# A graph network on one NeuronCore: block numbers of a chunk's groups loaded by one instruction at the chunk's head

## What is computed

```python
def forward(x):
    for layer in (transformer_conv, three_gat_convs, gatv2_with_kan, dot_attention):
        h = jnp.maximum(_layernorm(x, axis=-1), 0.0)
        x = x + layer(h)
    return x
# each edge layer, over all edges (src -> dst):
#   e     = score(node[dst], node[src])
#   alpha = exp(e - segment_max(e)[dst]); denom = segment_sum(alpha, dst)
#   out   = segment_sum(alpha[..., None] * value[src], dst) / denom
```

## Time and profile before

| | |
|---|---|
| median of 3 runs | 7453.76 us (7451.57 to 7457.46) |
| profiled execution, its own time | 7448.15 us |
| its span in the trace | 7446.4 us |
| granted TensorE clock, mean | 0.755 |
| TensorE busy | 4521.2 us (61%) |
| VectorE busy | 4569.1 us (61%) |
| ScalarE busy | 1779.9 us (24%) |
| GpSimd busy | 5124.9 us (69%) |

### The profile page before, as it was taken

How to read it: one execution, slowest core, us unless ns; L and a number is a source line. 1 busy time by engine, 2 the same in 40 slices (tenths; PEclk the granted TensorE clock), 3 DMA queues, 4 the chain that set the end, 5 groups by cost and what they waited for, 6 DMA issues and landing times. The chain is left out here.

```text
span 7446.4 us, 117629 instructions
## 1 busy us (share of the span) xinstructions
PE 4521.2 (61%) x21806; PEld 3437.6 (46%) x21806; DVE 4569.1 (61%) x15575; ACT 1779.9 (24%) x4978; POOL 5124.9 (69%) x5206
## 2 busy tenths in 40 slices
PE   3888887545555645555534444455766675677776
PEld 2544554433344433433433333444655564566665
DVE  5888887445555735555644444476777776566666
ACT  2888887200000000000010000043111111111111
POOL 5777773177777567777767777735777773777775
PEclk7999999777777767777766666666777777677677
DMA  3666664156666556666544444402444443566665
GB/s 88 164 166 165 163 165 129 41 178 184 187 185 185 164 164 186 187 185 183 183 121 135 138 132 132 138 30 66 129 130 130 129 130 99 173 184 180 181 182 154
DMA packets 659335, 1107.41 MB, mean 149 GB/s; under 512 B 233389, under 2 KB 383719, under 8 KB 658533
## 3 DMA queue, kind: packets, MB, share of 16 engines
q0 software_dynamic: 205312, 519.10, 26.9%
q1 hardware_dynamic: 450070, 579.16, 24.4%
q10 hardware_dynamic: 3280, 1.64, 0.1%
HBM read 997.90 MB, written 101.51 MB: 148 GB/s over the span
## 5 line engine op out<-in xcount | busy, mean ns | idle before, releaser
L516 POOL DMA_INDIRECT gat_ring<-tab,gat_ixb x2562 | 2459.8, 960 | 865.4 <-issue 738.3
L929 PE MATMUL gat_sc_ps<-gat_ring,gat_plain 128*128 128x264 f32 (+1 forms) x5124 | 1463.8, 430 | 42.9 <-DVE gat_ring L701 27.8
L516 POOL DMA_INDIRECT dot_ring<-tab,dot_ixb x854 | 831.5, 974 | 356.9 <-issue 237.7
L929 PEld LDWEIGHTS gat_sc_ps<-gat_ring,gat_plain 128*128 128x128 f32 x5124 | 985.1, 230 | 175.8 <-issue 83.4
L516 POOL DMA_INDIRECT conv_ring<-tab,conv_ixb x854 | 821.8, 962 | 310.0 <-issue 233.0
L516 POOL DMA_INDIRECT gatv_ring<-tab,gatv_ixb x854 | 838.0, 981 | 271.1 <-issue 244.2
L942 PE MATMUL gat_mx_ps<-ident,gat_lg 128*104 128x128 f32 x111 | 46.2, 416 | 1537.7 <-DVE gat_lg L757 1537.7
L746 DVE TENSOR_REDUCE gat_ex_sum<-gat_ex_ps 128x192 f32<-128x576 f32 (+1 forms) x114 | 81.8, 719 | 1428.8 <-SPq L525 1428.3
L701 DVE TENSOR_TENSOR gat_ring<-gat_ring,gat_p_ps 128x520 f32<-128x520 f32 (+1 forms) x1281 | 760.1, 594 | 4.1
L1052 ACT ACTIVATE gat_ring<-gat_low_own 128x96 f32<-128x96 f32 (+2 forms) x111 | 41.3, 372 | 2980.0 <-DVE gat_low_own L791 2783.6
L942 PEld LDWEIGHTS gat_mx_ps<-ident,gat_lg 128*104 128x104 f32 x111 | 17.7, 160 | 1570.4 <-issue 1570.4
(11 more groups left out here) (453 smaller groups left out, 7947.3 us busy)
## 6 DMA issues: line engine op xcount, KB each, us to landing
gat_plain<-d_plain SPq DMA_DIRECT2D x318, 512.0 KB
gat_turned<-d_turned SPq DMA_DIRECT2D x318, 256.0 KB
d_plain<-xs SPq DMA_DIRECT2D x427, 128.0 KB
gatv_plain<-d_plain SPq DMA_DIRECT2D x106, 512.0 KB
dot_plain<-d_plain SPq DMA_DIRECT2D x106, 512.0 KB
gat_ring<-tab,gat_ixb POOLq DMA_INDIRECT x2562
conv_rel_row<-d_rel SPq DMA_DIRECT2D x107, 256.0 KB
d_turned<-conv_ohT SPq DMA_DIRECT2D x427, 64.0 KB
```

The lines of the kernel that those rows point to most:

```text
L516: gp.indirect_dma_start(out=ring[:, r, t, 0:width], out_offset=None, in_=table[:, :], in_offset=bass.IndirectOffsetOnAxis(ap=ixb[:, r, t:t ...
L929: last = pe.matmul(sc_ps[:, m % SCB, 0:F], which[:, u, :], rows, start=(u == 0), stop=(u == 1))
```

## The change

In every layer but conv, TensorE and VectorE load the block numbers of all groups of a chunk with one instruction, values_load_multi_w_load_instructions, and keep them as values until the chunk is done with. The bounds 0 to 24 are given for it as before. TensorE does so in expand of the chunk's group 0; VectorE in shrink_sums of the chunk, whose own number is the first of them, and add takes its numbers from the list. In shrink_sums the load comes ahead of the wait for `shrink`, in conv too, where it stays a load of one number.

```diff
@@ message_pass
+    def blocks_of(ch, engine):
+
+        _, values = nc.values_load_multi_w_load_instructions(T.blk[0:1, BASE[ch]:BASE[ch + 1]], engines=[engine],
+                                                             min_val=0, max_val=NB - 1)
+        return values
+
@@ VectorE
+            block_at = {}
@@ add
                 m = BASE[i] + g
-                block_of = v.value_load(T.blk[0:1, bass.ds(m, 1)], min_val=0, max_val=NB - 1)
+                if conv:
+                    block_of = v.value_load(T.blk[0:1, bass.ds(m, 1)], min_val=0, max_val=NB - 1)
+                else:
+                    block_of = block_at[i][g]
                 v.wait_ge(s("scat"), m + 1)
@@ shrink_sums
+                if conv:
+                    block_of = v.value_load(T.blk[0:1, bass.ds(BASE[ch], 1)], min_val=0, max_val=NB - 1)
+                else:
+                    block_at.pop(ch - 2, None)
+                    block_at[ch] = blocks_of(ch, mybir.EngineType.DVE)
+                    block_of = block_at[ch][0]
                 v.wait_ge(s("shrink"), ch + 1)
-                block_of = v.value_load(T.blk[0:1, bass.ds(BASE[ch], 1)], min_val=0, max_val=NB - 1)
                 v.nop(nofuse=True)
@@ TensorE
+            block_at = {}
+
             def expand(i, r, g, use):
 
                 n = BASE[i] + g
-                block_of = pe.value_load(T.blk[0:1, bass.ds(n, 1)], min_val=0, max_val=NB - 1)
+                if conv:
+                    block_of = pe.value_load(T.blk[0:1, bass.ds(n, 1)], min_val=0, max_val=NB - 1)
+                else:
+                    if g == 0:
+                        block_at.pop(i - 1, None)
+                        block_at[i] = blocks_of(i, mybir.EngineType.PE)
+                    block_of = block_at[i][g]
                 mine = nd[:, bass.ds(block_of, 1), :].rearrange("p o w -> p (o w)")
```

## The result

Median of five runs 7491.3 us (7483.7 to 7494.2), against 7451.6 us (7443.4 to 7457.5) for the kernel before beside it: 40 us more, ratio 1.0054, 95% interval 1.0041 to 1.0066. The forecast was 7507 us, which is 53 us over the 7453.8 it started from; "slower" had the chance 0.75. The profiled run has a span of 7488.2 us, 41.8 more than the profiled run before, about the difference of the medians, so the two traces are laid side by side. Each is a single execution: conv, where only one load was moved, takes 1353.7 to 1358.8 us over the traces of before, the change and e1 to e8, so 1 or 2 us of a layer can't be told from nothing.

The account below looks back on a forecast made before the run. GpSimd's issue of gathers was taken to pace the five layers; gatv2's middle +27 and the tails +26 made +53 us, 7507 us on the 7453.76 median. The range was 7440 to 7780, the main case 7465 to 7560 (chance 0.42).

Parts of the forecast that it names:

- GpSimd's pace sets the middles: Five layers after conv: gather issue, 1.26 us a gather, paces them; TensorE and VectorE savings mid-layer are worth nothing.
- One load for n words, 0.31 + 0.057 a further word: Chunk heads on TensorE and VectorE: one load costs 0.31 us plus 0.057 us for each further word.
- Rival 1: Chunk heads: words load one after another, 0.305 us each; sum +386 us, 7840 us; chance 0.34.
- Checks kept, 0.28 us a number: Chunk heads, both engines: each number keeps its check and assert, about 0.28 us with gaps.
- gatv2, middle, +27: gatv2 before its tail: heads add 7.4 us a chunk against 6.6 available, short 0.8 in 34 chunks, +27 us.
- half of the 2.1 counts: gatv2's middle: of 2.1 us issue a chunk, half is recoverable, TensorE's clock being high about half the time.
- Rival 3: Heads are long but almost all covered, by gatv2's slack and tail waits for scatters: 7453 to 7469 us, chance 0.15.
- The prediction's slack: VectorE's idle time per chunk, taken as waits for gathered rows: 12.9 us in GAT, 8.6 dot, 5.6 gatv2.
- Tails, +26: Last four chunks: heads less removed issue and waits, 6.4 us gatv2, 5.7 dot, 6.9 each first two GAT, 0 third.
- Rest, 0: Conv, node stages, and GpSimd's and SyncE's queues: no cost or gain, 0 us.
- two thirds of rival 1's price: Cheaper further words in the heads: gatv2 gives 142 us, dot 10, tails 48; 7654 us.
- the tails give 20: Lower bound, load 0.31 us whatever n: gatv2's middle covered, 7474 us; upper, 0.1 us a word: tails 33, 7548 us.

Follow-up runs that it names:

- e1: The change taken back on VectorE, so only TensorE loads a chunk's numbers at the head: 7487.5 us, 1.0054 of the kernel before.
- e8: The change without bounds checks and asserts, each load widened to whole aligned groups of four words: 7421.2 us, 0.9951 of the kernel before.
- e6: The change with the row of block numbers starting one word later in SBUF: 7648.3 us, 1.0255 of the kernel before.
- e3: The change without any bounds check and assert of the five layers' block numbers: 7420.7 us, 0.9963 of the kernel before.
- e5: The change with each number checked where it is used instead of at the head: 7438.0 us, 0.9974 of the kernel before.
- e2: The change taken back on TensorE, so only VectorE loads a chunk's numbers at the head: 7473.4 us, 1.0035 of the kernel before.
- e4: The change with single checked loads again in VectorE's last five chunks and TensorE's last three of each layer: 7443.0 us, 0.9994 of the kernel before.
- e7: The kernel before, one number at a time, without checks and asserts of block numbers, conv's too: 7427.5 us, 0.9963 of the kernel before.
- e9: The change with loads widened to aligned groups of four words, all checks at the head: 1.0139 of the kernel before, which takes 8798 us beside it.
- e12: The same kernel as e9, run again: 1.0119 of the kernel before, which takes 8807 us beside it.
- e11: The change itself run again as a reference: 1.0171 of the kernel before, which takes 8798 us beside it.

## Why the prediction was right, and where not

**GpSimd's pace sets the middles:** right. First to last gather is unchanged in dot and gat2 and 4 to 6 us shorter in gat0 and gat1, though each chunk carries two heads of some 4 us; the shorter stretches are shorter gathers.

**One load for n words, 0.31 + 0.057 a further word:** 0.94 us forecast for twelve, 0.849 measured; right. For 7 and 6 words it gave 0.65 and 0.6, and they take 1.05 and 1.41 to 1.48: wrong, since the term has no alignment in it. The three short chunks of a tail thus cost VectorE some 2 us a layer more than the sum had. Rival 1 (0.305 us a word, 3.7 us) is refuted for these offsets; e6 shows that one word of offset brings three quarters of its load. The Trainium skill ("Runtime: NRT & Kernel Launch", Instruction fetch mechanics), with its 200 ns a register even in bulk, said of the register loads that the runtime puts in, gives an estimate of 12 x 0.2 = 2.4 us, near the unaligned 2.73 to 2.87 and far from the aligned 0.849; here the measurement decides.

**Checks kept, 0.28 us a number:** right. Ahead of gatv2's shrink, 0.85 + 12 x 0.28 = 4.21 against the 4.26 of the timeline; 1.05 + 7 x 0.28 = 3.0 against 3.09 for the chunk of seven. e3 and e5 show that these, in a row, are the price.

**gatv2, middle, +27:** this is a step that failed: "half of the 2.1 counts", because TensorE at 1.2 GHz would pace the catch-up, which left gatv2 "short by 0.8 us" a chunk. The first-to-last time grew by 10.1 us, of which 5.0 us are longer gathers, 3.0 bare issue of GpSimd and only 2.1 waits for scatters, the one part that a shortage of slack would make. Nor is the 10.1 that shortage in a smaller size: e1, with one head instead of two and so with slack to spare by the sum, has 9.2 of it, 8.2 of them in longer gathers. What was there to be had was 3.7 us a chunk of waiting for rows (182.4 to 45.6), 2.2 us of idle time ahead of the additions (85.2 to 3.1), whole and not half, and 1.2 us of busy time (645.6 to 609.4 us in 900 us, 29 chunks), since instructions that follow without a gap overlap more: an addition that started 0.19 us after its forerunner ended now starts 0.09 us before that. That is 7.1 us against two heads of 3.6 and 3.7. TensorE did not stand in the way: it pauses in the heads and runs the catch-up at 0.82 of full clock, mostly at 2.4 GHz. That the pause is what brings the higher clock was not tested; the rows show only that the one follows the other. Rival 3 had this mechanism for gatv2, at 0.15, but not for the tails. The prediction's slack was also misread: the 5.6 us a chunk in gatv2 and 8.6 in dot are all of VectorE's idle time before its first operation, of which waits for rows are 182.4/37 = 4.9 and 251.6/37 = 6.8. In dot the wait for rows fell by (251.6 - 131.2)/37 = 3.3 us a chunk, not 7, in GAT by 2.9, not 4; I take the reason to be the same small gaps.

**Tails, +26:** this term failed too, in size: the place is right, but the tails cost 41 to 46 us. The stretch that the sum priced, VectorE's from the head of the last full chunk to the layer's last addition, grew by 12.6 us in gat0 and 10.9 in gat1 (6.9 each forecast), 2.4 in gat2 (0), 8.0 in gatv2 (6.4) and 6.8 in dot (5.7): 40.7 us. Cut at the last gather it is 45.6, since in gat0 and gat1 the gathers ended some 4 and 6 us earlier and VectorE no sooner. The three short loads account for 2 us a layer. The rest is in GAT. There the sum took 2.2 us of waits and issue off the heads' 9.1, but the 1.4 us wait for rows among them ends at 2518.46 us, ahead of the first of these heads in gat0, and covers none of it; the heads cost 10.0 us in full. And VectorE waits 3.3 us longer for scatters in gat0 (1.5 to 4.8), which the sum had at nothing. TensorE's own heads are only a part of that: in e2, which has none, these waits are 3.8 us. In gat2 the waits set against the head did not cover all of it. That these tails are the loss, e4 shows: with single loads there they are back at 135.9 us of 136.0, and the time at 0.9994.

**Rest, 0:** right within the noise (conv 0.0, 2.7 us behind gatv2's tail, 3.3 us less ahead of the first gather).

So the number owes something to luck. Of the forecast's 53 us, 27 were to come from gatv2's middle and 26 from the tails; the 41.8 us measured are the tails' alone, and the middles sum to nothing. The tails came out 15 to 20 us over their term and gatv2's middle 17 under, and the two errors, with 10 us of shorter gathers in gat0 and gat1, nearly cancel. What was not luck is the sign and its reason: the checks, issued at a bare head, behind the last gathers.

Two slips in the working did not touch the forecast. At two thirds of rival 1's price dot would be short by 10.6 - 9.7 = 0.9 us in each of 34 chunks, some 30 us and not 10, which puts that case near 7670 us instead of 7654. And "the tails give 20" and "33" in the bounds come out nearer 19 and 31.

## What to carry to other kernels

Gathering register loads into one instruction is worth nothing that can be told where the numbers are unchecked (e7 against e3), and 19 us of 7457 where each is checked at its use (e5). What matters most is where the sequencer's checks land: a run of them at a point where nothing else covers them is paid in full, while the same checks one by one beside tensor work cost a fraction of it (e5 is 17 us over e8, which has none; the change, with them in a row, is some 77 over e8 by the ratios). In a kernel paced by one engine, price the tails first: work of the others behind its last instruction counts whole, the same work in front of it only beyond the slack. The slack can be more than the waits that the profile shows, as in gatv2, where the held-back VectorE caught up by dropping its small gaps.

## What the runs showed of the hardware

The time of a register load of several words depends on where they lie. From a start that is a multiple of four words, twelve take 0.849 us, eight 0.60 (e8), seven 1.05. From any other start, six take 1.41 to 1.48 and twelve 2.73 to 2.87 (e6). A load of one word takes 0.30 wherever it lies. As an estimate, some 0.07 us, plus 0.27 us for each whole group of four words from an aligned start and 0.235 us for each word left over, fits TensorE's times, if a load from any other start has no such groups at all (12 x 0.235 + 0.07 = 2.89). The last point is my reading of the sizes, but the short chunks of e6, which the estimate was not drawn from, bear it out (seven words from a start one off, 7 x 0.235 + 0.07 = 1.72, take 1.70; six from an aligned start, 0.07 + 0.27 + 2 x 0.235 = 0.81, take 0.82).

A bounds check of the sequencer is 183 to 190 ns on VectorE and 146 to 151 on TensorE, some three times the address arithmetic, which is the same kind of instruction (57 ns on VectorE, 46 on TensorE).

Beside e9 to e12, where the kernel before takes 18% longer, single instructions of the sequencers are now and then far longer. The checks of e11 have the same median as ever and reach 1.4 us:

```profile
L505 PEldq FUSED_REGOPS  x2135: 3/146/1397, 1767.5 to 8890.3; - x195
L505 PEldq SEQ_ASSERT  x2135: 2/18/1399, 1767.7 to 8890.5; - x195
```

The gathers themselves last what they always do there (972 ns in the mean, 987 in the change otherwise); the time between them grows (562.7 us of idle time in gatv2 for 276.3). What holds these runs back stays open. The change, with slack in gatv2 that is just enough otherwise, costs nearly four times as much there.
